# Routing constants, a folded bias and expert choice by chunks in an attention and mixture-of-experts layer

## The reference

```python
logits = xf @ Wg                                   # [n, 16]
_, topi = jax.lax.top_k(logits, 2)                 # two experts for each token
gates = jax.nn.softmax(jnp.where(mask, logits, -jnp.inf), axis=-1)
for e in range(16):
    h = jax.nn.silu(xf @ W1[e] + b1[e]) * (xf @ W11[e] + b11[e])
    y = y + (h @ W2[e] + b2[e]) * gates[:, e, None]
z = jax.nn.silu(xf @ Ws1 + bs1) * (xf @ Ws11 + bs11) @ Ws2 + bs2
return (y + z).reshape(b, t, d)                    # then the residual and the norm
```

## Time and profile before

| what | value |
|---|---|
| median of 3 runs | 726.2 us (724.15 to 727.62) |
| profiled execution, first to last instruction (span) | 723.0 us |
| TensorE clock granted, mean of the span | 0.944 of full speed |
| PE / PEld busy | 627.0 us (87%) / 511.7 us (71%) |
| DVE / ACT / POOL busy | 485.0 us (67%) / 417.0 us (58%) / 116.4 us (16%) |
| bytes by DMA | 33.57 MB, mean 46 GB/s |

### The profile page before, as it was taken

One profiled execution on the slowest core, in us unless ns is written; L12 is line 12 of the kernel. 1 busy time (PEld: TensorE's weight loads), 2 busy tenths in 40 slices (PEclk: granted clock), 3 DMA queues, 4 the chain that ended last, 5 costly groups with the idle time before them and its releaser, 6 DMA issues.

```text
span 723.0 us, 14787 instructions
## 1 busy us (share of the span) xinstructions
PE 627.0 (87%) x5300; PEld 511.7 (71%) x5300; DVE 485.0 (67%) x1556; ACT 417.0 (58%) x909; POOL 116.4 (16%) x229
## 2 busy tenths in 40 slices
PE   4899999999999999999999999998766079999930
PEld 2688888778888868888886888887623047888830
DVE  4788776698776778876768887767771033665636
ACT  4876566786655687665668766565330012655636
POOL 2000000000000000000000000000327600677630
PEclk9999999999999999999999999999599579999975
DMA  6600000130000040000007920003821100222233
GB/s 152 140 2 1 2 1 3 44 75 1 3 1 1 2 105 14 1 2 2 1 2 166 127 2 2 1 2 124 227 16 52 51 23 11 74 79 78 64 98 105
DMA packets 56393, 33.57 MB, mean 46 GB/s; under 512 B 23809, under 2 KB 49665, under 8 KB 56321
## 3 DMA queue, kind: packets, MB, share of 16 engines
q1 hardware_dynamic: 53760, 27.37, 18.8%
q0 software_dynamic: 2560, 5.26, 2.2%
HBM read 14.75 MB, written 9.48 MB: 34 GB/s over the span
## 4 chain that ended last, share of the span: by engine, by line
PE 74%; DVE 12%; another core or an unknown queue 5%; ACT 3%; issue 2%; DMA 2%; SPq 1%; POOL 0%; DVEq 0%; ACTq 0%; POOLq 0%
PE ps_t L966 18%; PE ps_o L1079 18%; PE ps_s L1048 11%; PE ps_s L1050 9%; PE ps_s L1198 5%; PE ps_o L1089 4%; PE ps_o L1186 3%; DVE k_l L671 3%; DVE q_hl L671 2%; PE ps_s L1122 2%; PE ps_t L1133 1%; PE ps_s L974 1%; ACT k_h L500 1%; DMA act_s<-y_rows 1%
## 5 line engine op out<-in xcount | busy, mean ns | idle before, releaser
L966 PE MATMUL ps_t<-ident,probs 128*128 128x128 f32 x1104 | 173.4, 275 | 11.6 <-ACT probs L512 11.5
L966 PEld LDWEIGHTS ps_t<-ident,probs 128*128 128x128 f32 x1104 | 134.9, 141 | 48.5 <-issue 11.4
L543 ACT ACTIVATE probs<-probs,nmax 128x128 f32<-128x128 f32 (+15 forms) x128 | 153.6, 1200 | 21.1 <-DVE nmax L766 12.4
L775 DVE COPY probsT<-ps_t 128x512 f32<-128x512 f32 (+3 forms) x160 | 91.3, 570 | 101.4 <-PE ps_t L966 100.4
L554 ACT ACTIVATE probsT<-ps_t 128x512 f32<-128x512 f32 (+3 forms) x160 | 89.7, 561 | 98.5 <-PE ps_t L966 97.1
L1048 PE MATMUL ps_s<-k_h,q_hl 128*128 128x512 f32 (+3 forms) x320 | 142.3, 448 | 0.4 <-DMA k_l<-k_l 0.4
L1079 PE MATMUL ps_o<-probsT,v_sb 128*64 128x128 f32 x2176 | 140.0, 277 | 1.3 <-DVE x_acc L790 1.2
L1079 PEld LDWEIGHTS ps_o<-probsT,v_sb 128*64 128x64 f32 x2176 | 116.8, 137 | 19.6 <-issue 14.6
L761 DVE TENSOR_SCALAR_CACHE_REDUCE probs<-ps_s 128x512 f32<-128x512 f32 x192 | 128.4, 686 | 0.7
L1050 PE MATMUL ps_s<-k_l,q_hl 128*128 128x512 f32 (+3 forms) x320 | 117.0, 366 | 0.0
L429 POOL TENSOR_TENSOR rden<-rsum,gate 128x2 f32<-128x2 f32 x64 | 12.6, 197 | 403.9 <-ACT probs L543 392.6
(11 more groups left out here) (144 smaller groups left out, 738.8 us busy)
## 6 DMA issues: line engine op xcount, KB each, us to landing
k_h<-k_h SPq DMA_DIRECT2D x32, 128.0 KB, 2.4
k_l<-k_l SPq DMA_DIRECT2D x32, 128.0 KB, 2.3
w_all<-in_L_ffn_W SPq DMA_DIRECT2D x2, 2048.0 KB, 12.6
xg<-x_sorted SPq DMA_DIRECT2D x48, 64.5 KB
x_sorted<-zeros SPq DMA_DIRECT2D x12, 256.0 KB, 9.5
act_s<-y_rows SPq DMA_DIRECT2D x8, 256.0 KB, 5.4
x_acc<-in_L_attn_tokens SPq DMA_DIRECT2D x4, 256.0 KB, 3.8
out<-x_acc SPq DMA_DIRECT2D x4, 256.0 KB, 2.3
```

Of the source, the lines that this page charges most:

```text
L543: nc.scalar.activation(probs[s % 2][h][:, 0:w], probs[s % 2][h][:, 0:w], ACT.Exp, bias=nmax[:, row], scale=-1.0, accum_out=rsum[:, row]).t ...
L775: nc.vector.tensor_copy(probsT[s % 2][h][:, c * BT:c * BT + w // P, :].rearrange("p n i -> p (n i)"), ps_t[1][:, 0:w]).then_inc(moved1, 1)
L966: return nc.tensor.transpose(dst, src, ident[:, :])
```

## The change

The second bias of the shared network, `bs2`, is no longer added by POOL to the normalised rows. It is loaded eight times into a second padded tile, `bs2_pad`, like `b2`, and POOL adds the two padded tiles once; since a token's gates add up to one, the matmul with `gatedT` then adds both. SP issues these loads and those of the shared weights behind the keys' copies of the first pair instead of ahead of them. POOL makes the routing constants early, right behind `out_weights(0)`. The experts are chosen in three sets of tiles (n0 and n1; n2; n3), each with its part of `hot` and `routed`, and PE turns n3 only after the logits of n2. `shared_act(0)` and `(1)` come after `slot`. `shared_add` takes the normalised rows as its second operand.

```diff
-            sp.wait_ge(b2_set, 1)
-            for k in range(GT8):
-                sp.dma_start(b2_pad[k * E:(k + 1) * E, k, :], b2).then_inc(b2_in, 16)
-            ... (the two columns)
-            sp.dma_start(bs2_all[:, :], bs2.rearrange("(a d) -> a d", a=1).to_broadcast([P, D])).then_inc(shw_in, 16)
-            ... (the three weight matrices)
             for x in START:
                 if x[1] == K:
                     k_across(x, start_high_of[x], start_fill_of[x] + ONE)
+
+            sp.wait_ge(b2_set, 2)
+            for k in range(GT8):
+                sp.dma_start(b2_pad[k * E:(k + 1) * E, k, :], b2).then_inc(b2_in, 16)
+                sp.dma_start(bs2_pad[k * E:(k + 1) * E, k, :],
+                             bs2.rearrange("(a d) -> a d", a=1).to_broadcast([E, D])).then_inc(b2_in, 16)
+            ... (the two columns, the three weight matrices)
@@ gpsimd
             nc.gpsimd.memset(b2_pad[:, :, :], 0.0).then_inc(b2_set, 1)
+            nc.gpsimd.memset(bs2_pad[:, :, :], 0.0).then_inc(b2_set, 1)
@@
             out_weights(0)
 
+            nc.gpsimd.iota(ie[:, :, :], pattern=[[0, NT], [1, E]], base=0, channel_multiplier=0,
+                           allow_small_or_imprecise_dtypes=True).then_inc(route_consts, 1)
+            nc.gpsimd.iota(it[:, :, :], pattern=[[1, SLOT_TILES], [0, E]], base=0, channel_multiplier=0,
+                           allow_small_or_imprecise_dtypes=True).then_inc(route_consts, 1)
+            nc.gpsimd.memset(counts[:, 0:1], 0.0).then_inc(route_consts, 1)
+            nc.gpsimd.memset(ones_row[:, :], 1.0).then_inc(route_consts, 1)
+            pool.wait_ge(b2_in, 16 * 2 * GT8)
+            nc.gpsimd.tensor_tensor(b2_pad[:, :, :], b2_pad[:, :, :], bs2_pad[:, :, :], ALU.add).then_inc(b2_summed, 1)
+
             pool.wait_ge(gate_ready, 1)
@@
             pool.wait_ge(acc_done, ONE + PAIRS * NT)
-            ... (the same iotas and memsets, on pool_step)
             nc.gpsimd.iota(rows[:, :, :, D].bitcast(i32), pattern=[[N, TOPK], [P, NT]], base=0,
                            channel_multiplier=1).then_inc(pool_step, 1)
-            pool.wait_ge(shw_in, 16 * 6)
-            for i, c in enumerate(NORM_ORDER):
-                cols = slice(c * BT, (c + 1) * BT)
-                pool.wait_ge(x1_ready, BT * (i + 1))
-                nc.gpsimd.tensor_tensor(shared[:, cols, :], rows[:, 0, cols, 0:D],
-                                        bs2_all[:, :].unsqueeze(1).to_broadcast([P, BT, D]), ALU.add).then_inc(shared_set, 1)
-            pool.wait_ge(pool_step, 8)
+            pool.wait_ge(pool_step, 4)
@@ vector, in largest_logits
+                for k in range(TOPK):
+                    ins = nc.vector.tensor_copy(idxf[:, k, cols], idx8[:, cols, k])
+                link(ins)
+                link(nc.vector.tensor_tensor(hot[:, :, cols, :], ... , ALU.is_equal))
+                nc.vector.tensor_tensor(routed[:, tiles[0] * E:(tiles[-1] + 1) * E] ... ,
+                                        hot[:, 0, cols], hot[:, 1, cols], ALU.add).then_inc(routed_ready, 1)
@@
-            largest_logits((n0, n1, n2), logit_bank(n2))
-            largest_logits((n3,), logit_bank(n3))
-            ... (idxf, hot and routed of all tiles)
+            dve.wait_ge(route_consts, 4)
+            largest_logits((n0, n1))
+            largest_logits((n2,))
+            largest_logits((n3,))
@@
             link(nc.vector.tensor_tensor_scan(tiles_end[:, :], ones_row[:, 0:E], tiles_n[:, :], 0.0, ALU.mult, ALU.add))
-            shared_act(0)
-
@@
-            shared_act(1)
@@
             nc.vector.tensor_copy(slot[:, :, :], slot_f[:, :, :]).then_inc(slots_ready, 1)
+            shared_act(0)
+            shared_act(1)
@@ shared_add
-            dve.wait_ge(shared_set, NC)
-                nc.vector.tensor_tensor(sh, ps_t[i % 2][:, :], sh, ALU.add).then_inc(shared_done, 1)
+                nc.vector.tensor_tensor(shared[:, cols, :], ps_t[i % 2][:, :].rearrange("p (n d) -> p n d", d=D),
+                                        rows[:, 0, cols, 0:D], ALU.add).then_inc(shared_done, 1)
@@ tensor
+            pe.wait_ge(acc_done, PAIRS * NT)
+            norm("logits", n2)
             norm("turn_x", n3)
-            norm("logits", n2)
             norm("logits", n3)
-            pe.wait_ge(shw_in, 16 * 6)
+            pe.wait_ge(shw_in, 16 * 5)
             shared_up(0)
-            pe.wait_ge(routed_ready, 1)
+            pe.wait_ge(routed_ready, 3)
@@
-                    pe.wait_ge(b2_in, 16 * GT8)
+                    pe.wait_ge(b2_summed, 1)
```

More of the change, by code:

```diff
@@ L249, in logit_bank @@
         def logit_bank(c):
-            return ps_t[1] if c == n3 else ps_s[0]
+            return {n2: ps_o[0], n3: ps_t[1]}.get(c, ps_s[0])
         def x_bank(i):
@@ L587, in _ @@
             norm("norm", n3)
-            act.wait_ge(shw_in, 16 * 6)
+            act.wait_ge(shw_in, 16 * 5)
             act.wait_ge(acc_done, ONE + PAIRS * NT)
@@ L723, in norm, with largest_logits @@
                                                 ALU.subtract, ALU.mult).then_inc(x1_ready, 1)
-            def largest_logits(chunks, bank):
+            def largest_logits(chunks):
                 tiles = range(min(chunks) * BT, (max(chunks) + 1) * BT)
@@ L729, in largest_logits @@
                 link(nc.vector.tensor_copy(logits[:, cols, :].rearrange("p n e -> p (n e)"),
-                                           bank[:, tiles[0] * E:(tiles[-1] + 1) * E]))
+                                           logit_bank(chunks[-1])[:, tiles[0] * E:(tiles[-1] + 1) * E]))
                 for t in tiles:
```

44 lines of the change are left out of this document (17 added, 27 removed).

## The result

The changed kernel took 732.48 us (median of 4 runs, 731.37 to 733.04), the kernel before 725.34 us (4 runs, 724.15 to 727.62): a ratio of 1.0083, 95% interval 1.0057 to 1.0109. The forecast was 729.7 us within 722 to 735, ratio 1.005. The profiled execution spans 730.6 us at a mean granted clock of 0.935, against 723.0 at 0.944.

What follows compares the result with a forecast made beforehand. PE was 87% busy, but a hole in all compute engines ended with the scatters, whose start hung on DVE's `slot` chain. Span 723.0 + 7.8 - 4.3 = 726.5 us, plus 3.2 gave 729.7 us, range 722 to 735.

Steps and rivals of the forecast that it cites:

- The start, +7.8 = 7.1 - 0.8 + 1.5: Early attention: DVE stands 7.1 us behind POOL's wait for late loads, 0.8 won back, 1.5 lost to half clock.
- the other early edits: Kernel start: second memset, early iotas and memsets, sooner key copies and later shared weights cost nothing.
- The end, -4.3 = -1.85 - 2.45: Routing after attention: routing matmuls start 1.85 us sooner, two shared steps leave the path to `slot` for 2.45.
- 5.6 as the bound: Routing after attention: largest gain forecast for the end, bounds being -2.9 and -5.6 us.
- Line 717 at 0.2 us: DVE's operation on four numbers a partition, before routing: 0.2 us instead of 2.79 once POOL's `bs2` adds go.
- rival d: Logits before routing: DVE's 3.5 us from POOL's adds reach PE whole, end gains 6.9, total 727.1 us; chance 0.05.
- The hole: Shared network beside scatters: about 30 us stall ending 3.6 us behind first `xg` load, then 28 to 29 us to experts.
- Rival (c): Hole opens by time from first scatter, putting 2 to 4 us more shared work behind release: 732.5 us; chance 0.13.
- Rival (e): Hole doesn't open or closes early, experts start at 575.7 instead of 610.3: about 699 us; chance 0.09.
- the 3.2 us that I put between span and time: Whole kernel: runs' median stands 3.2 us over the profiled span, untouched by the change.

Runs made afterwards that it cites:

- routing_first: Changed kernel with early bias and weight loads restored, and PE's `shared_up(0)` moved behind the two routing matmuls: 721.38 us, 0.9951 of the kernel before.
- old_choice: Changed kernel with early loads restored, experts chosen in two sets and n3 turned before n2's logits, as before: 724.98 us, 0.9971 of the kernel before.
- acts_back: Changed kernel with early loads restored, and `shared_act(0)` and `(1)` back inside the chain that makes `slot`: 724.84 us, 0.9997 of the kernel before.

## Why the prediction was right, and where not

**The start, +7.8 = 7.1 - 0.8 + 1.5.** Right. First reciprocal forecast at 43.2 us, measured 43.88; POOL's sum forecast at 2.35 us and ending at 42.45, measured 2.34 and 43.23. The attention segment grew by 7.1 us in one profile and by 8.0 in the other (486.2), with DVE's wait at 6.09 and 7.64: 7.5 on the mean. Taking POOL's wait away gives back 478.1. Beyond DVE's wait that is 1.0 and 0.4 us, where -0.8 + 1.5 had been forecast; the two terms apart weren't measured. Ahead of the wait two errors partly met: the last of the sixteen loads was issued at 39.21 us instead of 37.9, and had landed by 40.89, 1.7 us later instead of 2.2. The stretch of half clock behind it is there in both. What I put at nothing, "the other early edits", stayed nothing but for 0.2 us: the first scores came 1.6 us later in one profile and 0.2 in the other, and 1.4 us of that is the longer stretch of half clock ahead of them.

**The end, -4.3 = -1.85 - 2.45.** Right in sum and in what PE and DVE do, with a size off and a cause credited too much. At a like clock the last `x_acc` to the routing matmuls took 14.83 us instead of 16.50, so 1.67 for the forecast 1.85, and from there to `slot_f` 5.16 instead of 7.31, so 2.15 for the 2.45. That PE's `shared_up(0)` limits the first term was the judgement of the forecast, and routing_first shows it by gaining the 1.0 us behind it. But I put the term under the choice by chunks, and old_choice has 1.8 us of it without that choice. Wrong was to hold the 2.45 us for certain: 1.77 of them were partly DVE's wait for ACT, and acts_back, with the steps back in place, costs only 1.0 to 1.9, because its silu is ready when DVE comes to it. Where the clock comes back early the whole end gains 5.8 us, as in the first profile; I had given 5.6 as the bound, where its own terms, 2.9 and 2.45, add up to 5.35.

**Line 717 at 0.2 us**: 0.17. That its 3.5 us don't reach PE whole (rival d) holds for the changed kernel: at a like clock `routed` was whole 2.7 us sooner (13.71 us behind the last `x_acc` instead of 16.44; I had said 2.9), and the matmuls started 1.67 sooner. It holds through PE's new order alone: in the old one, in old_choice, the last logits start 2.4 us sooner.

**The hole.** The forecast that its end is tied to the end of the scatters, and that shared work of 28 to 29 us runs on behind it, came out (3.6 us behind `xg`, 29.2 us). Rival (c) is out for the change itself, since the hole opened at the same step, whose silu stood 13.3 us after the first scatter instead of 9.0. Rival (e) didn't come for the changed kernel on its chip, but on chip 1 there is no hole at all, in both profiles taken there. I had argued that it is there each time from three runs, all near 725 us. Chip 1 takes 41 to 44 us off both kernels and leaves the ratio, since without the hole too the experts wait for the scatters' end.

**The total.** Forecast +3.5 us; measured +6.0 (4.1 to 7.9) on the first chip and +4.2 (2.5 to 6.0) on chip 1. The second interval holds the forecast, the first doesn't quite. The terms as measured give 7.5 - 3.8 = +3.7, and up to 1.6 more ahead of the scores. Part of the nearness is luck: the span was forecast at 726.5 us and came to 730.6, 4.1 over, while the time is only 2.8 over, since the 3.2 us that I put between span and time were 2.1 in that run (2.1 to 2.9 in all four). The rest of the first chip's difference, some 1 to 2 us, I can't place: the profiles put 4.2 us into the experts, and that stage spreads by more without any change.

## What to carry to other kernels

Before a wait is put into a helper engine's program, look for the small result behind it that a busy engine takes in order: here a sum of 2.3 us whose result is wanted some 510 us later cost 7 us, and moved behind the gated sums of the first pair it left attention at its old 478.1 us. A step taken out of a chain is worth what the chain with the other edits loses to it, not the gap it had before. Two edits that shorten the same path may each give the whole gain alone; only undoing them one at a time, at a like clock, tells. And segments that a change doesn't touch must be compared across several profiles before a difference in them is called its effect.

## What the runs showed of the hardware that I had not expected

- The same program took 684 us on one chip and 725 to 727 on three or four others. In the two profiles of the changed kernel (42.3 us apart) the difference lies where POOL's indirect transfers run beside other work: 28.9 us from the first `xg` load to the first expert tile (32.8 against 3.9) and 15.5 among the experts. What makes PE's signals and the engines' next steps late there I can't say; that it needs the scatters, and that `past` doesn't open it, is what the runs show; with every `shared_down` behind the sixteen steps it comes later and in smaller waits, but isn't gone. Whether slower or fewer scatters at a time would avoid it wasn't tried.
- The half clock ahead of the first scores lasted 3.4 us in one profile of the changed kernel and 6.8 in the other, and moved them by 1.4 us.
- The 32 scatters take 39.4 to 40.1 us from the first to the last in every profile, on every chip.
- A DVE operation of 0.28 us took 2.43 us beside a POOL sum of the same length.
- Attention repeats at 478.0 to 478.2 us in the twelve profiles without POOL's early wait, while the routing from there to `slot_f` takes 17.2 to 20.0 us in seven profiles of one order, by the stretch in which the granted clock comes back.
